# The q/k/v stage of a macaron block: the gate's products first in each tile, those of v last, on TensorE and on ScalarE

## The reference

```python
q = silu(short_conv(x @ Wq + bq, q_conv)); q = q / (norm(q) + 1e-6)     # per head of 32
k = silu(short_conv(x @ Wk + bk, k_conv)); k = k / (norm(k) + 1e-6)
v = silu(short_conv(x @ Wv + bv, v_conv))                                # causal, 4 taps
alpha = sigmoid(x @ Wa + ba); beta = sigmoid(x @ Wb + bb)
out_gate = silu(x @ Wg + bg)
```

## Time and profile before

| | |
|---|---|
| median of three runs | 3779.1 us |
| the profiled execution's own time | 3778.79 us |
| its span | 3776.9 us |
| TensorE busy | 3342.2 us (88%) |
| VectorE busy | 2768.5 us (73%) |
| GpSimd busy | 1762.8 us (47%) |
| ScalarE busy | 1571.1 us (42%) |
| mean granted clock of TensorE | 0.955 |
| ScalarE in the q/k/v stage, one instruction each | table load 1.28 us, square of a tile 1.92, gate 0.68, silu 0.63, square root of the norms 0.59 |
| the gate's store, issue to landing | 6.5 us |

### The profile page before, as it was taken

The page is one execution under the profiler, slowest core; times in us unless marked ns, Lnnn a source line. Parts: engine busy times, 40 slices in busy tenths (PEclk is TensorE's granted clock), DMA queues, the critical chain, the costliest instruction groups (busy, mean ns, idle before and its releaser), DMA issues. The chain is left out here.

```text
span 3776.9 us, 196383 instructions
## 1 busy us (share of the span) xinstructions
PE 3342.2 (88%) x83728; PEld 2789.8 (74%) x83728; DVE 2768.5 (73%) x4434; ACT 1571.1 (42%) x2280; POOL 1762.8 (47%) x1664
## 2 busy tenths in 40 slices
PE   4999996799999999994999999999995764999999
PEld 3888885576767666663999999999994552888887
DVE  5676674677878787873888888888886664667665
ACT  2545542576767677670111111111112321544544
POOL 0332322456565555553777777777770000232332
PEclk9999998899999999997999999999997886999999
DMA  2212213132323232224666666666664443121221
GB/s 78 100 69 98 100 67 113 45 94 80 93 80 93 80 93 80 82 70 140 186 186 188 189 187 186 187 188 188 187 188 151 187 179 134 67 100 67 100 94 62
DMA packets 389849, 458.30 MB, mean 121 GB/s; under 512 B 65072, under 2 KB 365616, under 8 KB 365872
## 3 DMA queue, kind: packets, MB, share of 16 engines
q1 hardware_dynamic: 389808, 457.79, 38.1%
HBM read 337.03 MB, written 120.60 MB: 121 GB/s over the span
## 5 line engine op out<-in xcount | busy, mean ns | idle before, releaser
L262 POOL TENSOR_TENSOR ffn_out<-ffn_gate,ffn_xres 128x512 f32<-128x512 f32 x128 | 221.3, 1761 | 791.0 <-DVE ffn_gate L229 790.6
L604 DVE SCALAR_TENSOR_TENSOR ain_conv<-ain_padded,ain_taps,ain_conv 128x512 f32<-128x512 f32 x384 | 430.7, 1122 | 13.6
L1223 ACT ACTIVATE rec_yf<-rec_ps_f 128x256 f32<-128x256 f32 x129 | 49.6, 384 | 633.2 <-DVE rec_f_t L1154 633.2
L708 POOL TENSOR_TENSOR ain_conv<-ain_conv,ain_term 128x512 f32<-128x512 f32 x192 | 281.8, 1468 | 16.0
L1038 POOL TENSOR_TENSOR rec_d_norm<-rec_dmat,rec_early 128x512 f32<-128x512 f32 x131 | 166.9, 1274 | 202.0 <-DVE rec_dmat L1104 202.0
L1263 PE MATMUL rec_ps_scores<-rec_qk_pe,rec_kb 32*32 32x64 f32 x8320 | 143.8, 216 | 88.3 <-issue 45.8
L46 PE MATMUL ffn_ring<-ffn_mixkh,ffn_wkh 128*128 128x512 f32 x512 | 216.2, 422 | 0.0
L46 PE MATMUL ffn_ring<-ffn_mixrh,ffn_wrh 128*128 128x512 f32 x512 | 215.7, 421 | 0.0
L759 ACT ACTIVATE ain_buf<-ain_conv 128x512 f32<-128x512 f32 x192 | 121.0, 630 | 224.7 <-POOL ain_conv L708 127.2
L1263 PEld LDWEIGHTS rec_ps_scores<-rec_qk_pe,rec_kb 32*32 32x32 f32 x8320 | 126.6, 105 | 105.6 <-issue 105.6
L46 PE MATMUL ffn_ring<-ffn_act_h,ffn_wvh 128*128 128x512 f32 x512 | 201.7, 394 | 0.0
(11 more groups left out here) (239 smaller groups left out, 10284.0 us busy)
## 6 DMA issues: line engine op xcount, KB each, us to landing
rec_early<-coeffs SPq DMA_DIRECT2D x532, 96.0 KB, 2.3
rec_late<-streams SPq DMA_DIRECT2D x130, 384.0 KB, 3.4
streams<-ain_buf SPq DMA_DIRECT2D x48, 1024.0 KB, 5.1
rec_qk_pe<-streams SPq DMA_DIRECT2D x131, 256.0 KB, 3.1
rec_late<-coeffs SPq DMA_DIRECT2D x520, 64.0 KB, 2.2
rec_decay<-coeffs SPq DMA_DIRECT2D x532, 32.0 KB, 2.3
rec_early<-streams SPq DMA_DIRECT2D x133, 128.0 KB, 2.2
ffn_x<-in_x SPq DMA_DIRECT2D x16, 1024.0 KB, 8.4
```

Of the source, the lines that this page charges most:

```text
L262: last = nc.gpsimd.tensor_tensor(out[:, m, :], gate[:, m, :], xres[:, m, :], ALU.add)
L604: nc.vector.scalar_tensor_tensor(out=out[:], in0=pad[:, n:n + TOK], scalar=taps[:, u // KT, u % KT, n:n + 1], in1=out[:], op0=ALU.mult, op ...
L708: nc.gpsimd.tensor_tensor(out[:], out[:], term[:], ALU.add).then_inc(pool_conv, 1)
L1223: nc.scalar.activation(yf[:, 1], ps_f[:, :, 1, :], ACT.Copy).then_inc(f2_ready, 1)
```

## The change

TensorE computes the products in the order gate, q, k, v. ScalarE runs the four gate activations at the start of its tile, after the square of tile t+1, and no longer at its end; silu 11 now stands before the square root. The waits follow: the gate's products (u < 4) wait for shifts 8 to 11 of the tile before, the products of q (u = 4..7) for the gate's activations, the later ones for shifts. `biased` begins at 12, so every wait on it is 12 higher. The variance stays after u = 7, which is now q3. The head sums stand after u = 8..15, and `spread_rstd` after u = 11, which is now k3. The gate's store waits for four activations fewer. VectorE's, GpSimd's and SyncE's orders are the same.

```diff
@@ SyncE
-                sp.wait_ge(gate_ready, KT * t + 2 * KT)
+                sp.wait_ge(gate_ready, KT * t + KT)
@@ VectorE and GpSimd, convolve
-                dve.wait_ge(biased, 12 * t + u + 1)
+                dve.wait_ge(biased, 12 * t + u + 13)
-                pool.wait_ge(biased, 12 * t + u + 1)
+                pool.wait_ge(biased, 12 * t + u + 13)
@@ ScalarE, shift and slot
-                act.wait_ge(group_done, 16 * t + u + 1)
+                act.wait_ge(group_done, 16 * t + KT + u + 1)
...
                     square(t + 1)
+                act.wait_ge(gate_stored, 16 * t)
+                for m in range(KT):
+                    act.wait_ge(group_done, 16 * t + m + 1)
+                    nc.scalar.activation(gate[:, m, :], ring[m][:], ACT.Silu, bias=bias[:, 3, m:m + 1]).then_inc(gate_ready, 1)
                 for u in range(12):
...
                 silu(t, 10, more)
+                silu(t, 11, more)
                 act.wait_ge(heads_summed, 8 * t + 8)
                 nc.scalar.activation(inv_norm[HROWS, :], ps_rows[HROWS, :], ACT.Sqrt).then_inc(rooted, 1)
-                act.wait_ge(gate_stored, 16 * t)
-                for m in range(KT):
-                    if m == 2:
-                        silu(t, 11, more)
-                    act.wait_ge(group_done, 16 * t + 12 + m + 1)
-                    nc.scalar.activation(gate[:, m, :], ring[m][:], ACT.Silu, bias=bias[:, 3, m:m + 1]).then_inc(gate_ready, 1)
...
-            act.sem_inc(gate_ready, KT)
+            act.sem_inc(biased, 12)
@@ TensorE, slot
-                    if u < 4:
-                        pe.wait_ge(gate_ready, KT * t + u + 1)
+                    if 4 <= u < 8:
+                        pe.wait_ge(gate_ready, KT * t + u - 3)
                     else:
-                        pe.wait_ge(biased, 12 * t + u - 3)
-                    product(nc, ring[u % 4][:], *W["qkvg"[j]], m, xh[s], xl[s]).then_inc(group_done, 1)
-                    if 5 <= u < 13:
-                        head_sums(t, u - 5)
+                        pe.wait_ge(biased, 12 * t + u + 9 if u < 4 else 12 * t + u + 5)
+                    product(nc, ring[u % 4][:], *W["gqkv"[j]], m, xh[s], xl[s]).then_inc(group_done, 1)
                     if more and u == 7:
                         var(t + 1)
-                    if more and u == 10:
+                    if 8 <= u < 16:
+                        head_sums(t, u - 8)
+                    if more and u == 11:
                         spread_rstd(t + 1)
```

## The result

The changed kernel takes 4035.0 us (4034.1 to 4035.8, 4 runs), the kernel before in the same session 3778.8: a ratio of 1.068, 95% interval 1.066 to 1.070. The sign, the place and both mechanisms of the forecast (4085) were right; it was 50 us too high.

The account below looks back on a forecast made before the run. A closed loop through three GpSimd convolutions, not TensorE, bounds the q/k/v stage. Per period + 12.6 + 7.8 - 0.8 = + 19.6 us, 15 times 294, plus 11.8 in the last tile: + 306, so 4085 us; range 3975 to 4135.

Parts of the forecast that it names:

- both mechanisms of the forecast: q/k/v stage: gate products move into the loop ahead of q2, + 12.6 us; v0 queues behind the spread's wait, + 7.8 us.
- The closed loop: Per tile: mean, products to q2, three GpSimd convolutions with ScalarE's work between, then next mean: 63.6 us, the whole period.
- Gate products ahead of q, and the gate's queue: Tile start: four gate products and ScalarE's queue to the first gate delay q0; the loop grows by 12.6 us.
- The bounds of 11.2 and 16: For the 12.6 us term: 11.2 is products alone, 16 if norms, centring and table loads add 4 us.
- The spread: `spread_rstd` behind k3: TensorE waits about 10 us with v0 queued behind, so shift 8 and the loop grow by 7.8 us.
- The step that took the slow restart from one tile: Behind the spread's wait: the work takes 6.61 us at the low clock instead of 3.76, so shift 8 moves 7.8, not 5.0.
- The relief: GpSimd's convolution 8 runs faster while VectorE lacks v1: may gain 0 to 1.7 us, taken as -0.8 a tile.
- A sign that missed: If the forecast is right, TensorE is busy near 72% of the q/k/v stage.
- Rival 1: Only the gate products move into the loop and the spread's wait hides: 201 us more, 3980; chance 0.16.
- Rival 2: The gate's queue (norms, centring, square, table load) decides q0: 4 us more a tile, 4145; chance 0.13.
- Rival 3: Faster: TensorE's own work is the loop, and a mean ready before v3 ends gives its waits back: 3679; chance 0.03.
- The stores of the gate: Tile border: the gate's store lands about T + 11, ahead of the first gate at T + 17.5, hidden by 6 us.

Follow-up runs that it names:

- e3: Kernel before, ScalarE's order alone: alpha and beta behind shift 5 and ahead of silu 3, deviation behind shift 8 and ahead of silu 6: 3741.3 us, ratio 0.990.
- e8: Kernel before with 6 instead of 12 matmuls in each gate product: 3784.6 us, ratio 1.0017.
- e11: Kernel before with VectorE's convolution operations on 8 of 512 columns, GpSimd's work whole: 3679.1 us in a single run.
- e5: Changed kernel with the square root of the norms ahead of silu 11 again: 4031.1 us, ratio 1.067.
- e7: Changed kernel with the square root ahead of silu 11 and 6 instead of 12 matmuls in each gate product: 3978.0 us, ratio 1.053.
- e4: Changed kernel with 32 more matmuls per tile, results overwritten, ahead of the wait of `spread_rstd`: 4007.1 us, ratio 1.061.
- e1: Changed kernel with `spread_rstd` moved from behind k3 back to behind v2: 3936.5 us, ratio 1.042.
- e2: Kernel before with `spread_rstd` alone moved to behind k3, products in their old order: 3879.3 us, ratio 1.027.
- e6: Changed kernel with 6 instead of 12 matmuls in each gate product: 4062.8 us, ratio 1.076.

## Why the prediction was right, and where 50 us went

*The closed loop* held in every run of the table, and in e3 until another loop took over: e8 (cover), e3 (work taken out of the loop's links, not off TensorE, makes the kernel faster) and the table, in which the two links that the change does not touch (to shift 5, and from silu 8 to T) stay within 0.1 us in all kernels but e11.

*Gate products ahead of q, and the gate's queue*: 12.6 us forecast, 12.0 measured. In the tile shown the gate products began at T + 5.9, for 6.6, and ended at T + 17.3; q0 began at T + 17.7, after a wait of 0.38 for the gate, where 17.8 and 18.2 were forecast; e5 to e7 show both chains. The bounds of 11.2 and 16 held.

*The spread*: 7.8 forecast, 7.1 measured; the wait 8.4 us for about 10. (T + 56 less T + 44, the prediction's own two times, is 12 and not 10; no term of the sum hung on it.) k3 was done at T + 45, the spread began at T + 53.6 and not at T + 56: q0 came 0.5 us earlier, and the convolutions ahead of it gave back 1.5. The step that took the slow restart from one tile (6.61 us) was a little high; e4 measures the clock's part at 2.1 us for the 2.8 assumed.

*The relief* is the term that was mis-sized: 0.8 us forecast, 2.5 measured. The sentence that failed is that VectorE has the same work beside convolutions 2 and 5. For convolution 2 it has the same operations, but they fall elsewhere: in the mean of 14 tiles VectorE is busy for 8.6 of its 9.0 us before and for 5.5 of 8.2 in the changed kernel. Beside convolution 8 it is 9.1 of 9.2 and 4.3 of 8.2, which the prediction had foreseen, but priced at 0.8 and not at 1.0. Beside convolution 5 hardly anything changed, 5.4 of 8.8 and 5.1 of 8.2, and it still gained 0.6 us; what freed that is not shown. With the gate first, q0, q1 and q2 reach ScalarE at TensorE's pace (shifts 0 and 2 5.6 us apart, 3.8 before), and VectorE has finished convolutions 0 and 1 when GpSimd begins unit 2:

```profile
1196.01 2.33 DVE L604 SCALAR_TENSOR_TENSOR ain_conv<-ain_padded,ain_taps,ain_conv 128x512 f32<-128x512 f32 x3
1201.21 0.18 DVE L599 COPY ain_padded<-ain_tail 128x3 f32<-128x3 f32 x1 [2.87 <-ACT ain_conv L750]
```

Three operations in 2.33 us, alone, and then 2.87 us of idle VectorE from 1198.3, beside a convolution of GpSimd that starts at 1198.54. The sum: (12.6 - 12.0) + (7.8 - 7.1) + (2.5 - 0.8) = 3.0 us in each of 15 periods is 45 of the 50 us; 0.8 more is the last tile (11.0 us for 11.8). About 1.5 come from the table, whose 14 tiles grew by 16.6 us each where the 15 periods by `ps_ab` grew by 16.5. Some 2 us lie in the stages behind (2055.5 us after, 2057.7 before); they vary by as much between kernels that differ only in this stage, and no run explains it. The page of the Trainium skill "SBUF — State Buffer", section "Who interferes with whom", was set aside with 4.8 us as its most; that page has VectorE and GpSimd exclude each other at a port that they share. e11 shows that the one stretches the other, by 4.6 us in the three links, and the changed kernel got half of it back; that it is an exclusive lock no run here shows.

*A sign that missed.* TensorE was to be busy for 72% of the stage and was for 78%. The forecast kept its 946 us of busy time and made only the stage longer, although it counted on matmuls at the slow level. Measured are 48 us more for the same matmuls, in a stage that is also shorter than forecast.

*Rivals.* Rival 1 (the spread's wait hides) is refuted by e1 and e2. Rival 2 (the gate's queue decides) is refuted by e5, but the queue is as long as the other chain: cut TensorE's work alone and it does decide (e6). Rival 3, TensorE as the loop, is refuted by e8. The stores of the gate were hidden as forecast: the only wait for one is 4.9 us, in the last tile, where TensorE then waited 3.3 us for the gate.

## What to carry to other kernels

Find the closed loop before believing a busy share: an engine at 94% can be cover, and work that is moved from behind a loop's last link to ahead of its first is paid in full. When the order on an in-order engine changes, look at every wait that is written by position (`u == 11`): one that is three units earlier in terms of data puts the next product behind someone else's pace, here at a price of 40% of the whole loss. And price an idle neighbour: where VectorE and GpSimd run side by side, a delay for one gives time back to the other.

## What the runs showed of the hardware

- Less work on TensorE can cost time: 5.84 us of waiting put q0 on the slow spacing, 0.43 instead of 0.23 us, at a granted clock of 0.50, and e6's 15 periods grew by 19 us; 32 useless matmuls per tile gained 28 us in e4, where the same stretch ran at 1.00.
- A GpSimd convolution of three scaled additions on 128x512 (convolution 2, means of 14 tiles) took 7.4 us beside a VectorE busy for 4.0 of them with small operations (e11), 8.2 beside one busy for 5.5 (changed kernel) and 9.0 beside one busy for 8.6 (before). VectorE gains too: three of its operations took 2.33 us alone and up to 4.7 beside GpSimd.
